# Squares of the decays made by ScalarE as exponentials, in a hybrid layer on one core

## The reference, cut to what matters

```python
x_conv = _causal_depthwise_conv(x, conv_w, conv_b)
r_t = sigmoid(x_conv @ W_r.T + b_r)
i_t = sigmoid(x_conv @ W_i.T + b_i)
a_t = sigmoid(log_a) ** (8.0 * r_t)              # the decays
scale = sqrt(clip(1.0 - a_t * a_t, 0.0))
h = a_t * h + scale * (i_t * x_conv)             # a scan over the tokens
...
out = h @ W_out.T                                # then an RMS norm and the residual
```

## Time and profile before

| what | value |
|---|---|
| time, median of 3 executions | 1477.14 us (1476.16 to 1477.16) |
| the profiled execution's own time | 1475.19 us |
| its span, first to last instruction | 1473.3 us |
| mean granted TensorE clock | 0.941 of full speed |
| busy: PE, PEld | 1263.6 us (86%), 1015.7 us (69%) |
| busy: DVE, ACT, POOL | 980.9 us (67%), 737.3 us (50%), 678.5 us (46%) |

### The profile page before, as it was taken

The page is one execution under the profiler, slowest core; times in us unless marked ns, Lnnn a source line. Parts: engine busy times, 40 slices in busy tenths (PEclk is TensorE's granted clock), DMA queues, the critical chain, the costliest instruction groups (busy, mean ns, idle before and its releaser), DMA issues. The chain is left out here.

```text
span 1473.3 us, 17011 instructions
## 1 busy us (share of the span) xinstructions
PE 1263.6 (86%) x6050; PEld 1015.7 (69%) x6050; DVE 980.9 (67%) x1488; ACT 737.3 (50%) x1120; POOL 678.5 (46%) x533
## 2 busy tenths in 40 slices
PE   3499879999999999999959677898999999989871
PEld 1276658787878878787737555586787787778761
DVE  7787774577676576757979688954766566363632
ACT  3363444564645555474727353644473554645550
POOL 4325652336263544626848456644437055162204
PEclk9699989999999999999979898999999999999896
DMA  5000034434343343532110002022434434342243
GB/s 167 15 15 15 0 97 129 139 97 158 100 132 115 106 152 101 155 96 93 54 32 16 1 0 89 4 93 97 154 104 144 136 121 143 129 143 65 68 147 103
DMA packets 98371, 137.27 MB, mean 93 GB/s; under 512 B 9000, under 2 KB 83752, under 8 KB 98280
## 3 DMA queue, kind: packets, MB, share of 16 engines
q1 hardware_dynamic: 87408, 119.93, 25.5%
q0 software_dynamic: 4256, 10.24, 2.6%
q10 hardware_dynamic: 6624, 6.03, 1.2%
HBM read 119.64 MB, written 16.54 MB: 92 GB/s over the span
## 5 line engine op out<-in xcount | busy, mean ns | idle before, releaser
L495 POOL TENSOR_TENSOR rstd<-varis,half_neg 128x4 f32<-128x4 f32 x64 | 99.0, 1548 | 424.1 <-DVE varis L1777 239.7
L1348 PE MATMUL psum<-fwv,hid 128*128 128x256 f32 x1024 | 244.0, 384 | 14.7 <-ACT hid L814 14.4
L1348 PEld LDWEIGHTS psum<-fwv,hid 128*128 128x128 f32 x1024 | 196.3, 192 | 48.1 <-ACT hid L814 17.9
L1387 PEld LDWEIGHTS psum<-xst,ew 128*128 128x128 f32 x1472 | 181.5, 196 | 34.1 <-ACT xst L879 15.5
L1387 PE MATMUL psum<-xst,ew 128*128 128x128 f32 x1472 | 186.2, 281 | 18.4 <-ACT xst L879 10.9
L1395 PE MATMUL psum<-ew,hidt 128*128 128x256 f32 x736 | 169.8, 384 | 11.1 <-ACT hidt L885 11.1
L1395 PEld LDWEIGHTS psum<-ew,hidt 128*128 128x128 f32 x736 | 139.6, 192 | 37.3 <-ACT hidt L885 14.2
L1260 PE MATMUL psum<-ident,xhat 128*128 128x128 f32 x376 | 58.0, 306 | 75.6 <-POOL xhat L499 68.7
L1260 PEld LDWEIGHTS psum<-ident,xhat 128*128 128x128 f32 x376 | 49.4, 159 | 84.4 <-issue 60.0
L602 POOL DMA_INDIRECT xs<-xf_rows,token_of_slot x46 | 60.8, 1322 | 100.5 <-PE psum L1375 87.8
L885 ACT ACTIVATE hidt<-psum 128x512 f32<-128x512 f32 x92 | 54.9, 597 | 96.7 <-PE psum L1387 96.2
(11 more groups left out here) (221 smaller groups left out, 2745.2 us busy)
## 6 DMA issues: line engine op xcount, KB each, us to landing
ew<-in_w SPq DMA_DIRECT2D x92, 1024.0 KB, 5.4
rows_ring<-in_x SPq DMA_DIRECT2D x14, 512.0 KB, 5.0
out<-rows_ring SPq DMA_DIRECT2D x14, 512.0 KB, 7.7
ys_rows<-ys ACTq DMA_DIRECT2D x46, 128.0 KB, 4.7
xf_rows<-ew SPq DMA_DIRECT2D x2, 1024.0 KB, 4.4
xf<-in_x SPq DMA_DIRECT2D x2, 512.0 KB, 4.5
space<-in_f_w_key SPq DMA_DIRECT2D x1, 1024.0 KB, 7.4
fwv<-in_f_w_value SPq DMA_DIRECT2D x1, 1024.0 KB, 9.9
```

The lines of the kernel that those rows point to most:

```text
L495: pool.tensor_tensor(dst, src, half_neg[:, 0:src.shape[1]], ALU.pow).then_inc(done, 1)
L1348: last = nc.tensor.matmul(rows4[:, k, :], hid[:, j % NHID, k * P:(k + 1) * P], fwv[:, j, :], start=j == 0 and k % 2 == 0, stop=j == FC - 1 ...
L1387: last = nc.tensor.matmul(bank_e[:, j * P:(j + 1) * P], ew1[:, c, at:at + P], xst[:, c, :], start=c == 0, stop=c == DC - 1)
```

## The change

`decays` gets two more `Exp` behind the two that it has, with the columns `log_a8 = 2 * log_a4` as scale and bias: they write `a^2` straight into `om`. `scales` loses its first instruction and waits for the squares in place of the decays; what it keeps makes `min(a^2 - 1, -TINY)`, the negated complement, and `root_of` undoes the sign with `scale=-1.0` in its `Ln`. The start gets one more tiny DVE instruction for `log_a8`. It holds for all 16 runs.

```diff
-LOG_STEPS = 6 + len(LOG_TERMS) - 1 + 3
+LOG_STEPS = 6 + len(LOG_TERMS) - 1 + 4
...
+        log_a8 = sb("log_a8", [P, DC])
...
+        squares = steps("squares", numbered("q", DC), B)
-        rec_om = steps("rec_om", ["na", "om"], B)
+        rec_om = steps("rec_om", ["om"], B)
...
             def decays(p):
...
+                for c in range(DC):
+                    nc.scalar.activation(s.om[:, c, :], s.rg[:, c, :], ACT.Exp, bias=log_a8[:, c:c + 1],
+                                         scale=log_a8[:, c:c + 1]).then_inc(squares.sem, 1)
...
             def root_of(p):
...
-                nc.scalar.activation(s.om[:], s.om[:], ACT.Ln).then_inc(root.sem, 1)
+                nc.scalar.activation(s.om[:], s.om[:], ACT.Ln, scale=-1.0).then_inc(root.sem, 1)
...
                 step(nc.vector.scalar_tensor_tensor(log_a4[:], q, -8.0, t, ALU.mult, ALU.add))
+                step(nc.vector.tensor_scalar(log_a8[:], log_a4[:], 2.0, None, ALU.mult))
...
             def scales(p):
                 s = rec_sets[set_of(p)]
-                dve.wait_ge(decays_made.sem, decays_made.count(p, "a1"))
-                nc.vector.scalar_tensor_tensor(s.om[:], s.aa[:], -1.0, s.aa[:], ALU.mult, ALU.mult).then_inc(rec_om.sem, 1)
-                dve.wait_ge(rec_om.sem, rec_om.count(p, "na"))
-                nc.vector.tensor_scalar(s.om[:], s.om[:], 1.0, TINY, ALU.add, ALU.max).then_inc(rec_om.sem, 1)
+                dve.wait_ge(squares.sem, squares.count(p, "q1"))
+                nc.vector.tensor_scalar(s.om[:], s.om[:], -1.0, -TINY, ALU.add, ALU.min).then_inc(rec_om.sem, 1)
```

## The result

The changed kernel took 1487.59 us (median of 4 executions, 1486.11 to 1488.23) beside 1476.65 us (median of 4) for the kernel before: a ratio of 1.0075, 95% interval 1.0058 to 1.0093, so 10.9 us slower. The forecast was 1487.7, in a range of 1482 to 1493. The profiled execution took 1487.94 us, its span 1486.0 against 1473.3 before.

What follows compares the result with a forecast made beforehand. PE bounds turns 4 to 8; in turns 9 to 12 DVE is busier. 9.9 + 0 + 0.6 - 2.5 + 0 + 2.4 + 0.2 = +10.6 us on 1477.14 gives 1487.7 us, range 1482 to 1493.

Steps and rivals of the forecast that it cites:

- Seven turns: Turns 4 to 8, 13 and 14: squares delay `norm_in`, on which PE's weight load waits without slack; 1.41 us each, 9.9 us.
- Rival B: In the seven turns another wait with its own clock absorbs PE's delay: they give 0, 1477.8 us; chance 0.07.
- rival D: The seven turns cost about 0.7 us each, half the price: 1482.7 us; chance 0.10.
- Turn 9: PE's output product comes 1.41 us later, but PE then waits 7.80 us for POOL's rows: 0.
- Turn 10: ACT's `inverse`, now behind the squares, becomes the late one, where DVE was late by 0.8 us: +0.6 us.
- Turns 11 and 12: Runs 7 and 8: squares fit into ACT's idle time before `Ln`, L1914 leaves the path: -1.25 us each, -2.5 us.
- Tail: Last three runs of the recurrence: the squares delay the root where ACT's idle time is too short; sum +2.4 us.
- Run 13: In the tail: ACT idled 0.88 us before `Ln`, which takes up part of the squares' 1.41 us: +0.4 us.
- run 14: In the tail: nothing idles between `decays`, `conv_in`, the root and `rows_back`, for which PE waits: the full +1.4 us.
- run 15: In the tail: ACT idled 0.78 us before `Ln`; the rest, about +0.6 us, passes through the waiting Gelu to PE.
- Rival A: The new gaps also lower PE's clock: another 1.7 us in each of the seven turns, 12 more, 1500 us; chance 0.08.
- Rival C: All DVE time of five runs in turns 9 to 12 leaves the path, POOL shrinks too: -3.9, 1473.2 us; chance 0.03.

Runs made afterwards that it cites:

- e1: Changed kernel with the squares behind `norm_in` instead of in front of it in the turns of the usual pattern: 1480.30 us, ratio 1.0025 to the kernel before.
- e3: Kernel before plus a further pair of `Exp` behind the decays in all 16 runs, into an unread buffer, VectorE as before: 1489.29 us, ratio 1.0091.
- e5: Changed kernel plus a second pair of `Exp` in front of the squares in all 16 runs, into an unread buffer: 1513.26 us, ratio 1.0251.
- e4: Kernel before without VectorE's squaring, the complement made of the decays themselves in one instruction, ScalarE as before: 1464.88 us, ratio 0.9922.
- e2: Changed kernel with ScalarE's squares in runs 7 and 8 alone; VectorE squares in the other fourteen: 1473.13 us, ratio 0.9982 to the kernel before.
- e8: Kernel before with VectorE's squaring left out in runs 13 to 15 alone: 1473.39 us, ratio 0.9978.
- e7: e1 with run 5's squares (turn 9) put back in front of `norm_in`: 1477.34 us, ratio 1.0006 to the kernel before.
- e6: e2, and in runs 13 to 15 VectorE squares each chunk when its decays are there: 1468.39 us, ratio 0.9946 to the kernel before.

## Why the prediction was right, step by step

- **Seven turns, 7 x 1.41 = 9.9 us: right in mechanism and size.** The rows give 1.43 a turn, 10.0 in all once run 9's product is taken off. PE's wait by its products was 1.13 us and not the 1.4 that I had named as the sign; by its loads it was 1.53, and the turns grew by the full price. e1 moved the pair behind `norm_in` and turns 4 to 8 gave back all of it; e3 has the same cost with VectorE untouched; e5 doubles it. Rival B (absorbed) and rival D (half) fell with the first row.
- **Turn 9 at 0: right**, and by the step's own reason. The same instructions of PE stand 9.30 us apart in the two traces in front of it and 9.28 behind it; its output product waits 2.77 us, the wait for GpSimd's rows 6.29 instead of 7.80. e4 shows the other half: with `norm_in` in its old place the turn gives 1.4 us.
- **Turn 10, +0.6.** `gated` starts 0.64 us later than the shift so far, as ScalarE's `inverse` is now the late one; 0.4 to 0.5 are left at the end of the turn, since a product behind took 5.75 us for 6.08.
- **Turns 11 and 12, -2.5.** ScalarE's idle time in front of `Ln` is 2.26 us in turn 11:

```profile
876.29 1.06 ACT L867 ACTIVATE space<-space 128x1024 f32<-128x1024 f32 x1 [2.26 <-DVE space L1920]
```

2.7 shorter than in the earlier trace rows, and PE's block comes 1.25 us sooner in turn 11 (its wait is 6.17 us for 7.43) and 1.28 sooner by VectorE's list in turn 12. In turn 12 the idle time is 2.52 us, only 1.4 shorter, and not the 2.7 forecast: PE's products in front had regained 1.3 us of clock and brought ScalarE's list there sooner. Not in the forecast: the clock then gave 0.7 us more in turn 12 and took 1.3 back in run 9's product, which took 6.64 us for 5.30 behind a wait of the same 6.75 us.
- **Tail, +2.4: 0.5 too much.** Run 13 cost 0.40 and run 14 1.41, as worked out; run 15's 0.58 reached the Gelu. In front of it PE waited 1.4 us longer for `rows_back(c)` (3.11 us for 1.70), which the forecast had not seen and the wait for the Gelu took up. Behind it the clock alone decided: three products took 3.78, 3.72 and 3.63 us for 3.15, 5.54 and 2.05, together 0.5 less.
- **Start, +0.2: not shown.** The changed kernel's profile is 2.1 us behind by turn 3, but e2, with the same link in the chain, is 0.1 behind, and e8, without it, 1.2. Whatever the link costs is under what executions differ by.
- **Rival A (the clock pays too) fell at this gap and comes true three times in seven at twice the gap.** Seven of seven output products took 3.72 us behind a wait of 1.13; behind 2.54, three of seven took 1.5 to 1.7 more. The example from which the rival took its price doesn't hold by itself either. The product of turn 11 in the earlier trace rows, in the changed kernel, behind the same wait:

```profile
907.39 3.69 PE L1283 MATMUL psum<-wo,dec 128*128 128x256 f32 x16 [2.05 <-DVE dec L1866]
```

So it is in eight of the ten kernels (3.69 us); only the kernel before and e8 have 5.38. The 1.69 us are no gain, for PE then waits as much longer for VectorE (4.63 us for 2.95). The case that the Trainium skill describes ("TensorE: Matmul & The Clock Gate", section "HAM oscillation") has waits longer than the bursts of products between them. The prediction read it more widely than that: PE is busy for 412.7 of 427 us in turns 4 to 8, and its gaps of 1.13 us cost no clock.
- **Rival C (faster) fell, but VectorE's relief was worth more than I thought**: 11.1 us alone, against the 1.9 that I saw in turns 10 to 12. The change could not have it, since its own squares took it back: in turn 9 by `norm_in`, in the tail by the root; and the copy of turn 11 stayed caught (3.12 us).
- **The total is closer than its parts, and that is luck.** 10.9 us were measured for 10.6. The clock gave 0.7 us in turn 12 and 0.5 in the tail and took 1.3 in run 9's product, none of which the forecast had; that these cancel to 0.1 is chance. The place in front of `norm_in`, 10.0 of the 10.9, is no luck.

## What to carry to other kernels

Before work is handed to a half-idle engine that runs in order, look at what is queued behind the new place and who waits for that: here 1.41 us stood in front of the one instruction that PE took up 0.05 us later, seven times, while the same pair one place further down cost nothing in any of the seven (in turn 9, another turn, it cost 2.8 us by way of VectorE and GpSimd). Relief of VectorE paid only where the trace shows somebody idle and waiting for it; here two runs of sixteen by moving the work (2.8 us), and three more by splitting it so that its first half starts sooner. Where VectorE and GpSimd work side by side, a shift of under 1 us can cost or earn more than 2 us, so read their neighbouring rows again after each move.

## What the runs showed of the hardware

- A VectorE instruction of 0.75 us (128x512, two inputs) takes 2.84 to 3.20 us when one of GpSimd's begins beside it, and a copy of 0.69 us 3.12. In turn 9 of e1 two were caught instead of one, which with a start 0.7 us later cost the turn 2.8 us; e7 gave it back. Not every one is caught: `y<-psum,y` (L1865, one input in PSUM) began at 738.75 under GpSimd's L567 (738.42, 2.63 us long) and took its usual 1.21 us. Sparing one can mean that the next is caught: in turn 10 of e3 the squaring took its usual 1.23 us and not 3.33, but the complement behind it took 2.76 for 0.69, and GpSimd's product beside them 3.45 for 2.38.
- Behind a wait of 1.13 us PE's clock held seven times in seven, behind 2.54 four times in seven. Behind 2.05 us in turn 11 it held in eight kernels of ten. In the tail the product of run 14 took 3.79 us (before, wait 4.39 us in front of its group; 3.78 in e2 with 4.38) or 2.05 (e6 with 4.41, e8 with 4.66, e4 with 4.67). A tail of long waits thus carries a lottery of 1.7 us a product, which turned 0.9 to 1.3 us of worked-out gain into 3.8 to 4.1 in the profiles; by which rule a gap falls on either side these runs don't settle.
